# Hosting the last node pair: all of its even batches in the third edge-score pass, its odd batches in the first and the fourth dense slot pass, taken two turns sooner

## The reference, cut to what matters

```python
def _sage_layer(h, edge_src, edge_dst, W, b):
    msg_sum = segment_sum(h[edge_src], edge_dst, n)
    m = msg_sum / maximum(deg, 1.0)[:, None]
    return relu(concatenate([h, m], axis=1) @ W + b)
h = _sage_layer(x, src, dst, W1, b1)
h = _sage_layer(h, src, dst, W2, b2)
x = _layernorm(x + h)
```

## Time and profile before

| what | us |
|---|---|
| median of 3 runs (5068.57 to 5076.53) | 5069.83 |
| the profiled execution | 5069.27 |
| its span, first to last instruction | 5067.3 |
| PE busy in it | 3921.8 (77%) |
| DVE busy | 3812.1 (75%) |
| ACT busy | 3449.9 (68%) |
| POOL busy | 3019.2 (60%) |
| mean granted TensorE clock | 0.910 |

### The profile page before, as it was taken

The page is one execution under the profiler, slowest core; times in us unless marked ns, Lnnn a source line. Parts: engine busy times, 40 slices in busy tenths (PEclk is TensorE's granted clock), DMA queues, the critical chain, the costliest instruction groups (busy, mean ns, idle before and its releaser), DMA issues. The chain is left out here.

```text
span 5067.3 us, 107533 instructions
## 1 busy us (share of the span) xinstructions
PE 3921.8 (77%) x23992; PEld 2869.7 (57%) x23992; DVE 3812.1 (75%) x14850; ACT 3449.9 (68%) x11317; POOL 3019.2 (60%) x2914
## 2 busy tenths in 40 slices
PE   2999999566997799994998974997876676665554
PEld 1666766344775455773555752444766565665554
DVE  5899999676998787897886966997758787444433
ACT  0899999554886576894776863887878787333332
POOL 2888888475552122761224462887757676767777
PEclk9999999787998899997999997998999899997666
DMA  1556666587997576994777984675766665543332
GB/s 62 164 185 198 200 194 190 177 283 250 348 351 254 175 242 207 350 363 155 241 240 240 336 298 144 226 226 169 232 203 209 190 208 185 156 146 116 93 100 70
DMA packets 606698, 1061.18 MB, mean 209 GB/s; under 512 B 109736, under 2 KB 130874, under 8 KB 606508
## 3 DMA queue, kind: packets, MB, share of 16 engines
q1 hardware_dynamic: 524780, 920.61, 53.1%
q0 software_dynamic: 81728, 138.51, 10.6%
HBM read 608.75 MB, written 453.92 MB: 210 GB/s over the span
## 5 line engine op out<-in xcount | busy, mean ns | idle before, releaser
L2534 POOL DMA_INDIRECT got_c<-table,src_row x980 | 931.5, 951 | 387.8 <-issue 292.9
L1428 POOL DMA_INDIRECT src_got_s<-table,src_row x588 | 554.6, 943 | 439.1 <-issue 93.5
L2566 PE MATMUL bank<-pick_c,got_c 128*128 128x128 f32 x1960 | 334.0, 324 | 360.1 <-DMA got_c<-table,src_row 293.0
L2076 PE MATMUL bank<-w_all,dt_m 128*128 128x512 f32 x1176 | 568.7, 600 | 34.7 <-DMA dt_m<-delta_t 33.1
L2566 PEld LDWEIGHTS bank<-pick_c,got_c 128*128 128x128 f32 x1960 | 289.6, 227 | 402.1 <-issue 245.8
L2050 POOL TENSOR_TENSOR part_m<-part_m,half_sum_m 128x512 f32<-128x512 f32 x98 | 158.7, 1619 | 580.7 <-DVE half_sum_m L2283 580.7
L1601 ACT ACTIVATE z_s<-z_s,shift_s,dev_s 128x128 f32<-128x128 f32 x1080 | 443.9, 485 | 2.5 <-DVE shift_s L1739 1.3
L791 PEld LDWEIGHTS bank<-w_mean,ht 128*128 128x128 f32 x2352 | 312.1, 193 | 142.9 <-issue 142.9
L2590 PE MATMUL bank<-w_c,agg_c 128*128 128x128 f32 x1960 | 367.9, 313 | 5.6 <-ACT agg_c L2711 5.3
L2711 ACT COPY agg_c<-bank 128x512 f32<-128x512 f32 x245 | 142.6, 582 | 328.3 <-DVE bank L1914 280.2
L788 PE MATMUL bank<-bias,first_row 128*128 128x512 f32 x588 | 321.9, 629 | 38.0 <-ACT ht L851 14.3
(11 more groups left out here) (352 smaller groups left out, 11913.3 us busy)
## 6 DMA issues: line engine op xcount, KB each, us to landing
table<-rows SPq DMA_DIRECT2D x294, 256.0 KB
x_s<-table SPq DMA_DIRECT2D x270, 256.0 KB
x_c<-table SPq DMA_DIRECT2D x245, 256.0 KB
table<-z_s SPq DMA_DIRECT2D x196, 256.0 KB
table<-z_c SPq DMA_DIRECT2D x196, 256.0 KB
table<-mid_s SPq DMA_DIRECT2D x172, 256.0 KB
own_rows_s<-table SPq DMA_DIRECT2D x147, 256.0 KB
pick_t_s<-picks_t SPq DMA_DIRECT2D x147, 256.0 KB
```

The lines of the kernel that those rows point to most:

```text
L1428: nc.gpsimd.indirect_dma_start(out=src_got[r][:, g, :], out_offset=None, in_=tables[l].rows, in_offset=bass.IndirectOffsetOnAxis(ap=src_ro ...
L2076: nc.tensor.matmul(b_h[k % n_h][:, :], dt[b.slot][:, k, :], w_all[:, l, :, :].rearrange("p h d -> p (h d)"), start=True, stop=True).then_i ...
L2534: nc.gpsimd.indirect_dma_start(out=got[r][:, g, :], out_offset=None, in_=t_in.rows, in_offset=bass.IndirectOffsetOnAxis(ap=src_row[:, t:t ...
L2566: ins = nc.tensor.matmul(b_sum[r][:, k * P:(k + 1) * P], got[b.slot][:, k, :], pick[r][:, k, :], start=k == 0, stop=sage, skip_group_check ...
```

## The change

The third edge-score pass becomes one block with one node batch in each turn, for all 49 slot batches: the even node batches 0 to 96. The first dense slot pass hosts the odd ones from 49 to 97, as before (`spare` is 49). The fourth dense slot pass, `convolve(3)`, sage with ReLU, hosts the odd ones from 1 to 49, 25 of them. In both hosting passes the steps of a hosted batch are taken two turns sooner (its load three), so the streams end two turns earlier. In the diff an offset of 4 that becomes 2 is such a step.

```diff
 (SP)
-                            b = at(3)
+                            b = at(0)
                             if even(b):
                                 load_nodes(b)
...
-                            b = at(6)
+                            b = at(4)
                             if even(b):
                                 store_node_middle(b)
-                            b = at(9)
+                            b = at(7)
                             if even(b):
                                 store_nodes(b)
-                        skewed(sp, nb, 9 if nodes else 6 if norm else 4, step, 4)
+                        skewed(sp, nb, 7 if nodes else 6 if norm else 4, step, 4)
...
 (PE)
                         def node_steps(at):
-                            b = at(4)
+                            b = at(2)
                             if even(b):
                                 node_middle(b)
-                            b = at(5)
+                            b = at(3)
                             if even(b):
                                 node_product(b)
-                            b = at(3)
+                            b = at(1)
                             if even(b):
                                 node_hidden(b)
...
                             b = at(2)
                             if b:
                                 product(b)
+                            b = at(0)
                             if even(b):
                                 node_turn(b)
...
 (ACT)
                         def node_steps(at):
-                            b = at(3)
+                            b = at(1)
                             if even(b):
                                 node_relu(b)
+                            b = at(2)
+                            if even(b):
+                                node_middle_out(b)
                             b = at(4)
                             if even(b):
-                                node_middle_out(b)
-                            b = at(6)
-                            if even(b):
                                 node_deviation(b)
-                            b = at(7)
+                            b = at(5)
                             if even(b):
                                 node_normalise(b)
...
-                            b = at(2)
+                            b = at(0)
                             if even(b):
                                 node_turned(b)
...
 (DVE)
-                            b = at(6)
+                            b = at(4)
                             if even(b):
                                 node_scale(b)
...
-                            b = at(5)
+                            b = at(3)
                             if even(b):
                                 node_residual(b)
                                 node_moments(b)
...
 (the passes)
-        middle = (nb + 1) // 2
+        spare = nb // 2 * 2 + 1
...
-        edge_scores(2, third[3], third[4], *third[0:3], 0, middle)
-        edge_scores(2, third[3], third[4], *third[0:3], middle, nb, True)
+        edge_scores(2, third[3], third[4], *third[0:3], 0, nb, True)
...
-        convolve(0, ..., third + (2 * (nb - middle) + 1,))
+        convolve(0, ..., third + (spare,))
...
-        convolve(3, "sage", False, ...)
+        convolve(3, "sage", False, ..., third + (1,))
```

More of the change, by code:

```diff
@@ L2680, in _ @@
                         if sage:
-                            skewed(pe, nb, 5 if nodes else 3 if norm else 2, step_sage_norm if norm else step_sage_relu, 4)
+                            skewed(pe, nb, 3 if nodes or norm else 2, step_sage_norm if norm else step_sage_relu, 4)
                         else:
-                            skewed(pe, nb, 5 if nodes else 2, step_gcn_norm if norm else step_gcn_relu, 4)
+                            skewed(pe, nb, 3 if nodes else 2, step_gcn_norm if norm else step_gcn_relu, 4)
                     @block.scalar
@@ L2812, in _ @@
                         else:
-                            skewed(act, nb, 7 if nodes else 2 if sage else 1, step_relu, 4)
+                            skewed(act, nb, 5 if nodes else 2 if sage else 1, step_relu, 4)
                     @block.vector
@@ L2945, in _ @@
                         else:
-                            skewed(dve, nb, 6 if nodes else 2, step_relu, 4)
+                            skewed(dve, nb, 4 if nodes else 2, step_relu, 4)
         t = tables + [final]
@@ L2966, in program @@
         attend(1)
-        middle = (nb + 1) // 2
+        spare = nb // 2 * 2 + 1
         third = (t[6], t[7], t[8], (io["L3_gnn_W1"][0:D, :], io["c_L3_gnn_b1"]), (io["L3_gnn_W2"][0:D, :], io["b_L3_gnn_b2"]))
-        edge_scores(2, third[3], third[4], *third[0:3], 0, middle)
-        edge_scores(2, third[3], third[4], *third[0:3], middle, nb, True)
+        edge_scores(2, third[3], third[4], *third[0:3], 0, nb, True)
         softmax(2)
         attend(2)
-        convolve(0, "gcn0", False, t[3], t[4], None, (io["L1_gnn_W1"],), io["b_L1_gnn_b1"], third + (2 * (nb - middle) + 1,))
+        convolve(0, "gcn0", False, t[3], t[4], None, (io["L1_gnn_W1"],), io["b_L1_gnn_b1"], third + (spare,))
         convolve(1, "gcn0", True, t[4], t[5], t[3], (io["L1_gnn_W2"],), io["b_L1_gnn_b2"])
         convolve(2, "gcn1", True, t[5], t[6], t[5], (io["L2_gnn_W"],), io["b_L2_gnn_b"])
-        convolve(3, "sage", False, t[6], t[7], None, (io["L3_gnn_W1"][D:, :], io["L3_gnn_W1"][0:D, :]), io["b_L3_gnn_b1"])
+        convolve(3, "sage", False, t[6], t[7], None, (io["L3_gnn_W1"][D:, :], io["L3_gnn_W1"][0:D, :]), io["b_L3_gnn_b1"], third + (1,))
         convolve(4, "sage", True, t[7], t[8], t[6], (io["L3_gnn_W2"][D:, :], io["L3_gnn_W2"][0:D, :]), io["b_L3_gnn_b2"])
```

## The result

The changed kernel takes 5255.15 us (median, 5248.81 to 5258.43), the kernel before 5070.30 on the same chip: a ratio of 1.0361, 95% interval 1.0346 to 1.0377. It is slower by 3.6%. I had forecast 5206, slower by 2.7%, with a range of 5140 to 5275. The direction and the mechanism held. The size did not: the time is that of the third rival, in which the clock falls in both gaps (5261).

The account below looks back on a forecast made before the run. Pace was taken from the touched passes: edge-score turns, the fourth dense pass bound by POOL's gathers until PE waits on ACT's order. 5069.3 - 71.1 - 5.4 + 158 + 55 = 5206 us, slower by 2.7%, range 5140 to 5275.

Parts of the forecast that it names:

- the third rival: Fourth dense pass: PE's clock falls in both gaps of a pair; 5261 us, to 5347 if it hardly returns; chance 0.23.
- The edge-score pass: Third edge-score pass as one block: 48 intervals of 5.46 us, 261.9 in place of 333.0, so 71.1 us less.
- The first dense pass: Its end: the last hosted residual comes two turns sooner, the 2.03 us wait on a store stays; 5.4 us less.
- The loop of waits in the fourth dense pass: PE waits each turn for ACT's agg behind hosted steps: a pair takes 16.1 us, not 10.0; pass 158 more.
- Fill and end: Fourth dense pass outside its 24 pairs: some 13 us before them and 16.4 after, to the next first gather.
- PE's clock: Fourth dense pass: one clock fall in a pair, 2.3 us each, 55 us in all; bounds 0 and 196.
- the odd gap: PE's idle time in odd fourth-pass turns, from node_hidden until ACT has done relu, normalisation and three copies: 3.83 us.
- The even gap: PE's idle time in even fourth-pass turns, from node_middle until agg, through second bias and deviation: 3.04 us.
- The transfers: Fourth dense pass: the hosted batches' stores and loads, 75 DMAs of 256 KB, cost nothing.
- Rival 1: Fourth dense pass keeps the gathers' pace, a pair of 10.0 us, only the end 11.4 longer; 5004 us; chance 0.08.
- Rival 2: Fourth dense pass: the same loop of waits, but PE's clock stays up, without the 55; 5151 us; chance 0.17.

Follow-up runs that it names:

- the shift alone: The change's sooner hosted steps, but with the kernel before's division of node batches (nothing hosted in the fourth dense pass): 5064.46 us, ratio 0.9979 to the kernel before.
- three filling matmuls: The change in its order, but PE runs three matmuls with overwritten results ahead of the product in each fourth-pass turn: 5159.85 us, ratio 1.0161 to the kernel before.
- the odd gap alone: The change, but ACT's three copies for agg stand ahead of hosted steps in the fourth pass's even turns only: 5130.34 us, ratio 1.0098 to the kernel before.

## Why the prediction was right, and where it was off

- **The edge-score pass**, 71.1 less: 69.5, right.
- **The first dense pass**, 5.4 less: 7.2, and 7.1 with the shift alone. The direction is right; that exactly the 2.03 wait stays was a guess.
- **The loop of waits in the fourth dense pass**, a pair of 16.1 at full clock in place of 10.0: 16.11 with the clock held up. It was summed from rows of another pass and of one single turn, and it came out exact, since each link is a fixed duration on one engine in a fixed order. Fill and end, 29.4: 17.5 to the first product and 14.0 from the last (4735.11) to the next gather, 31.5.
- **PE's clock**, 55: this is the term that was mis-sized. First to last product are 482.9 us, 96.5 over 24 times 16.1. I took "one fall in a pair, at the odd gap, which exceeds 2.7 clearly". The even gap (3.04 in my sum, 2.87 to 2.96 in the trace) exceeded it too, and I gave the few tenths between them the weight of a reason. The one gap that I had measured told when the clock fell there; I used it as if it told when it must fall. With 97 in place of 55 the sum is 5248, and with the 10.3 before the third edge-score pass, which no edit made, 5258; the profiled execution took 5258.43.
- **The transfers**, nothing: 3 us with them alone. Right within what counts.
- **Rival 1** (the pass keeps the gathers' pace) needed the copies ahead of the hosted steps. Given that order, its price, a longer end of 11.4, is what was measured: 11.3. **Rival 2** (the clock stays up) was wrong for the change; it is the run with three filling matmuls, 5160 against its 5151. **Rival 3** was what happened: 5261 against 5255.

Both products of a pair at half clock behind gaps of 3.78 and 2.87: by the Trainium skill, "TensorE: Matmul & The Clock Gate", section "HAM oscillation — how this bites in real kernels", an array that waits some 3 to 5 us for data between its bursts starts every burst cold. The change's trace agrees at 3.78, and shows the same at 2.87, just under those waits (two falls a pair would be 110 by my price for one; measured 96.5). The run with the odd gap alone does not agree: 8 of 23 products behind 3.78 started at full clock.

What a fall costs hangs on who sets the pace. The fifth dense pass runs at a clock of 0.75 now in the stretch shown, and 0.68 before in the same part of the pass (4571.5 to 5011.5; the 0.66 of the earlier trace rows is of a later part), and takes 507 us either way. There POOL is the bound: in 440 us it is busy for 335 and issues for 104, before and now, so what PE's clock does is free. In the fourth pass PE stands in the loop itself, so each microsecond of its product counts.

## What to carry to other kernels

Idle time of an engine is of use to guest work only if the guest does not hold up what the host loop waits for in the same turn. Here two statements in the other order turned +3.6% into -1.2%. Where the host loop has a turn to spare, the guest may stand ahead: in the first dense pass ACT's copies are made a turn before PE's product, and that pass takes 266.6 with its 25 guests, the two after it (of other layers) 262.3 in the mean without any. So follow one full turn through all streams, as a sum of links, before you count shares of busy time. And where a loop leaves TensorE idle for 2 us or more in each turn, carry both clock levels to the range, not a threshold from one gap.

## What the runs showed of the hardware that I had not expected

- How long an idle gap must be for the clock to fall was not one number. With gaps of 1.70 and 1.21 it never fell in the stretches read; with 2.06 in 9 of 14 pairs; with 2.26 and 2.9 in some pairs and not in others of the same kernel; and even at 3.78 one product of 23 ran at full clock to its end. With 2.06 and 2.26 the falls came after PE had started again, never ahead of the product. With an even gap of 2.95 in a steady loop of 13.7 us, the moment of the fall moved slowly through the pairs. The runs don't show what it is counted from.
- A fall inside the product costs about as much early as late: behind gaps of 2.06, 8.39 with the fall in the first row (0.77) and 8.41 with it in a later one (4309.07 to 4317.48), where 6.75 is the length without.
- Matmuls that compute nothing of use made the change 95 us faster (5255 to 5160), by keeping the clock at 2.4 GHz.
